# Attention: the products of probabilities and values of a batch, taken one step later

## The chip, the core and the metric

The kernel runs on one core of a Trainium2 chip. That core has TensorE (PE, the matrix engine, with its weight loads shown apart as PEld), VectorE (DVE), ScalarE (ACT), GpSimd (POOL) and SyncE (SP, which here only issues DMAs). Each engine takes its own instructions strictly in the order in which the program wrote them, and waits on semaphores that other engines raise. The metric is the device time in microseconds (us) of one execution; the time of a kernel is the median of several executions.

## The reference

Four parts run one after another on `x` of 16 batches x 512 rows x 256 columns: attention with a layer norm and a residual, a mixture-of-experts feed-forward, a Mamba mixer, and the feed-forward again. Only the attention is touched:

```python
Q = x @ Wq.T + bq;  K = x @ Wk.T + bk;  V = x @ Wv.T + bv        # x is the normed input
theta_q = Q * inv_wl + phase_bias;  theta_k = K * inv_wl + phase_bias
sim = cos(theta_q) @ cos(theta_k).T + sin(theta_q) @ sin(theta_k).T
weights = softmax(sim / sqrt(256), axis=-1)
out = weights @ V                                                # x + out goes on
```

## The kernel before

The function `attention` handles the 16 batches one after another. There is no planner: for each engine a function `emit(st)` writes the instructions of one step, and `run_steps` calls it for steps -3, -2, ... and then in a loop. In the step of batch b, `st.has(1)` guards work for batch b+1, `st.has(2)` for b+2 and so on; `st.has(0)` is the batch itself. So the order of the sections inside `emit` is the order of the queue of that engine. The stages of a batch are:

- **Load and norm.** SP loads `xin` (L163). DVE takes the statistics (L270 to L277), POOL the power -0.5 (L188), DVE writes the normed `xn` (L301). These are done three steps ahead.
- **Transposes.** PE transposes `xn` into the banks `ps_t` (L412), DVE splits them into a high and a low part `xT_hi`, `xT_lo` (L261, L264). Two steps ahead, at the end of the step on PE.
- **Projections.** PE makes four blocks of queries and keys (L376) and two blocks of values (L384), one after another in two PSUM banks that take turns, `ring[0]` and `ring[1]`. ACT empties the first four into `theta` (L319), DVE the last two into `vals` (L229). Block three needs the bank that ACT has emptied of block one. One step ahead, at the start of the step on PE.
- **Angles.** DVE reduces `theta` into one turn with five passes (L236 to L251). ACT then makes sine, absolute value and cosine (L341, L342, L345) and two rounded copies `trig_hi` (L347, L350), and POOL and DVE the two remainders `trig_lo` (L194, L219). One step ahead up to the copies.
- **Similarities.** PE makes four blocks of `ps_s` with 48 matmuls (L401). ACT takes the exponential of each into `probs` (L329), in the order: the four `theta` of batch b+1, the four exponentials of batch b, the sines and copies of batch b+1.
- **Probabilities times values.** PE makes four blocks `ps_o` (L424), each of 257 columns, in two banks that take turns; the last column is the sum of the probabilities. DVE divides and adds the residual (L288, L290), SP stores (L173).

On PE the step of batch b is: projections of b+1, similarities of b, transposes of b+2, products of b. In text below, "block three" is the third block of projections, and "the products" are always the matmuls of L424. `probs`, `vals`, `xres`, `xout`, `trig_hi` and `trig_lo` each have two buffers. The attention is followed by the first feed-forward, which starts when the last batch is stored.

Of the kernel before, what the change touches and what calls it, by code (L numbers as in the profile page):

```python
# [54 lines left out]
def attention(nc, x, wqkT, wvT, bqk, bv, phase, inv_wl, ident, x1):  # L55
# [8 lines left out]
    C1 = 6.28125  # L64
    C2 = 2.0 * math.pi - C1
    PI_IN = 3.1415925
    with ExitStack() as ctx:
        def sb(name, shape, dt=F32):
            return ctx.enter_context(nc.sbuf_tensor("a_" + name, shape, dt))
# [78 lines left out]
        def _(sp):  # L148
# [8 lines left out]
            def emit(st):  # L157
                if st.has(3):
                    h, n = st.half(3), st.turn(3)

                    if st.reuses(3):
                        sp.wait_ge(xn_ready, TT * (st.item(3) - 1))
                    sp.dma_start(xin[h][:, :, :], rows(x, st.item(3))).then_inc(xin_loaded[h], 16)  # L163
                if st.has(0):
                    h, n = st.half(0), st.turn(0)

                    if st.reuses(0):
                        sp.wait_ge(out_free[1], 2 * (st.item(0) - 1))
                    sp.dma_start(xres[h][:, :, :], rows(x, st.item(0))).then_inc(xres_loaded[h], 16)

                    for r in range(2):
                        sp.wait_ge(out_free[r], 2 * st.item(0) + 2)
                    sp.dma_start(rows(x1, st.item(0)), xout[h][:, :, :]).then_inc(stored[h], 16)  # L173

            run_steps(sp, emit, NB, 3)
            for h in range(2):
                sp.wait_ge(stored[h], 16 * (NB // 2))

# [21 lines left out]
        def _(dve):  # L200
# [13 lines left out]
            def emit(st):  # L214
                if st.has(0):

                    h, b = st.half(0), st.item(0)
                    dve.wait_ge(trig_high, 2 * b + 2)
                    nc.vector.tensor_tensor(trig_lo[h][:, NF:2 * NF, :], trig[:, NF:2 * NF, :],  # L219
                                            trig_hi[h][:, NF:2 * NF, :].bitcast(F32),  # L220
                                            ALU.subtract).then_inc(cos_low, 1)
                if st.has(1):
                    h, n, b = st.half(1), st.turn(1), st.item(1)

# [41 lines left out]
                if st.has(3):  # L266
# [6 lines left out]
                    for t in range(TT):  # L273
# [2 lines left out]
                    dve.wait_ge(mv_done, b + 1)  # L276
                    nc.vector.tensor_scalar(var_eps[h][:, :], mv[h][:, :, 1], EPS, None,  # L277
                                            ALU.add).then_inc(var_done, 1)
                if st.has(0):
                    h, n, b = st.half(0), st.turn(0), st.item(0)  # L280
                    dve.wait_ge(xres_loaded[h], 16 * (n + 1))

                    if st.reuses(0):
                        dve.wait_ge(stored[h], 16 * n)
                    for t in range(TT):
                        r = t % 2
                        dve.wait_ge(out_full[r], 2 * b + t // 2 + 1)
                        nc.vector.reciprocal(rden[:, t:t + 1], ps_o[r][:, D:D + 1]).then_inc(rden_done, 1)  # L288
                        dve.wait_ge(rden_done, TT * b + t + 1)
                        ins = nc.vector.scalar_tensor_tensor(out=xout[h][:, t, :], in0=ps_o[r][:, 0:D],  # L290
                                                             scalar=rden[:, t:t + 1], in1=xres[h][:, t, :],
                                                             op0=ALU.mult, op1=ALU.add)
                        ins.then_inc(out_free[r], 1)
                if st.has(3):
                    h, n, b = st.half(3), st.turn(3), st.item(3)
                    dve.wait_ge(rstd_done, b + 1)
# [5 lines left out]
                                                      rstd[h][:, t:t + 1], ALU.subtract, ALU.mult)  # L302
                        ins.then_inc(xn_ready, 1)

            run_steps(dve, emit, NB, 3)

        @block.scalar
        def _(act):
# [47 lines left out]
        def _(pe):  # L356
# [9 lines left out]
            def emit(st):  # L366
                if st.has(1):
# [11 lines left out]
                    for v in range(2):  # L379
                        r = take(st, NF + v)  # L380
                        for u in range(2):
                            t = 2 * v + u
                            for i, (wp, xp, k) in enumerate(parts):
                                ins = nc.tensor.matmul(ring[r][:, u * D:(u + 1) * D],  # L384
                                                       xp[:, k, t * P:(t + 1) * P], wp[:, k, 2 * D:3 * D],
                                                       start=(i == 0), stop=(i == len(parts) - 1))
                        ins.then_inc(ring_full[r], 1)
                if st.has(0):
                    h, n, b = st.half(0), st.turn(0), st.item(0)

# [13 lines left out]
                if st.has(2):  # L404
                    h, b = st.half(2), st.item(2)
                    pe.wait_ge(xn_ready, TT * (b + 1))
                    for k in range(KT):
# [4 lines left out]
                            ins = nc.tensor.transpose(ps_t[k][:, t * P:(t + 1) * P],  # L412
                                                      xn[h][:, t, k * P:(k + 1) * P], id_sb[:, :])
                        ins.then_inc(xT_full, 1)
                if st.has(0):
                    h, b = st.half(0), st.item(0)
                    pe.wait_ge(probs_ready, TT * (b + 1))
                    for r in range(2):
                        pe.wait_ge(ring_free[r], 3 * b + 3)
                    for s in range(TT):  # L420
                        r = s % 2
                        pe.wait_ge(out_free[r], 2 * b + s // 2)
                        for t in range(TT):
                            ins = nc.tensor.matmul(ps_o[r][:, 0:D + 1], probs[h][:, t, s * P:(s + 1) * P],  # L424
                                                   vals[h][:, t, :], start=(t == 0), stop=(t == TT - 1))
                        ins.then_inc(out_full[r], 1)

            run_steps(pe, emit, NB, 3)

AXIS = mybir.AxisListType
# [1348 lines left out]
```

## Time and profile before

| | |
|---|---|
| median of 3 executions | 3050.72 us (3048.64 to 3051.18) |
| profiled execution, its own time | 3049.55 us |
| its span | 3047.7 us |
| mean granted clock of TensorE | 0.949 of full speed |
| attention | from the start to about 508 us |
| PE busy over the whole span | 2680.0 us (88%) |
| DVE, ACT, POOL busy over the whole span | 2345.8, 1847.0, 1824.2 us |

A row of the timeline gives start, duration, engine, line, operation, output<-input, shape and count; a bracket at its end is the idle time of the engine before it and what ended it. L401 is line 401 of the kernel before. A matmul of f32 operands counts as two in the records (an `x16` of L424 is eight matmuls of the program).

### The profile page before, as it was taken

What the parts mean: (1) busy time and instruction counts of PE and PEld (TensorE: products, weight loads), DVE (VectorE), ACT (ScalarE), POOL (GpSimd) and SP (SyncE); (2) the same over time, 40 slices, a digit from 0 to 9 for tenths busy, and PEclk for the clock granted to TensorE, in tenths of its full rate; (3) what the DMA queues carried; (4) which work ended last, traced back from release to release, by engine and by line L of the source; (5) the groups of instructions that cost most, each with busy time, mean ns of one, the idle gap of its engine ahead of it and who ended that gap; (6) DMA issues with size and microseconds to landing.
All of it is one profiled execution on the core that took longest, in us unless ns stands there. A gap on an engine that the chain in (4) does not pass through costs nothing. (4 is left out here: it accounts for less than half of the span.)

```text
span 3047.7 us, 48452 instructions
## 1 busy us (share of the span) xinstructions
PE 2680.0 (88%) x17374; PEld 2139.6 (70%) x17374; DVE 2345.8 (77%) x2432; ACT 1847.0 (61%) x2523; POOL 1824.2 (60%) x1211
## 2 busy tenths in 40 slices
PE   5999995795389999999999999999999999985793
PEld 4877874563158788788787787787887877874562
DVE  6888874463259898898988998988989989895563
ACT  3565562252178677776776776676777767761451
POOL 1221220454148778777777787787877877784454
PEclk8999998798599999999999999999999999997896
DMA  1121213323222021120220210202202202103423
GB/s 48 63 62 41 62 49 73 108 77 89 77 70 63 15 84 43 42 84 8 77 85 1 84 59 26 84 14 72 84 2 83 70 15 77 43 29 80 119 77 100
DMA packets 137178, 186.01 MB, mean 61 GB/s; under 512 B 27848, under 2 KB 112712, under 8 KB 136968
## 3 DMA queue, kind: packets, MB, share of 16 engines
q1 hardware_dynamic: 129480, 162.68, 17.3%
q0 software_dynamic: 7488, 20.46, 2.6%
q8 instruction: 141, 2.31, 0.3%
q14 instruction: 69, 0.57, 0.1%
HBM read 141.12 MB, written 41.98 MB: 60 GB/s over the span
## 5 line engine op out<-in xcount | busy, mean ns | idle before, releaser
L1287 POOL TENSOR_TENSOR m_state<-m_state,m_c_all 128x1024 f32<-128x1024 f32 x512 | 1204.5, 2366 | 358.8 <-DVE m_state L1379 357.7
L1379 DVE TENSOR_TENSOR_SCAN m_state<-m_decay,m_ps_d 128x1024 f32<-128x1024 f32 x512 | 1161.9, 2278 | 149.9 <-issue 88.8
L1447 ACT ACTIVATE m_decay<-m_dt,m_aneg 128x511 f32<-128x511 f32 x1024 | 657.6, 710 | 27.4 <-DVE m_state L1379 26.6
L1671 PEld LDWEIGHTS m_ps_d<-m_bdiag,m_duT 128*128 128x128 f32 x4096 | 491.8, 193 | 109.8 <-issue 77.3
L1671 PE MATMUL m_ps_d<-m_bdiag,m_duT 128*128 128x128 f32 x4096 | 508.1, 278 | 33.3 <-DVE m_state L1379 23.7
L1684 PE MATMUL m_ps_y<-m_ident,m_state 128*128 128x128 f32 x4096 | 534.2, 274 | 2.8 <-POOL m_state L1287 2.5
L1684 PEld LDWEIGHTS m_ps_y<-m_ident,m_state 128*128 128x128 f32 x4096 | 464.7, 142 | 8.4 <-POOL m_state L1287 7.3
L1356 DVE TENSOR_TENSOR m_duB<-m_duT,m_ps_i 128x1024 f32<-128x1024 f32 x256 | 306.0, 1195 | 7.7 <-ACT m_duT L1475 7.7
L1669 PEld LDWEIGHTS m_ps_d<-m_ident,m_duB 128*128 128x128 f32 x2048 | 235.6, 141 | 76.8 <-issue 70.8
L1669 PE MATMUL m_ps_d<-m_ident,m_duB 128*128 128x128 f32 x2048 | 265.8, 273 | 7.1 <-DVE m_state L1379 7.0
L1585 PE MATMUL m_ps_f<-m_hT,m_win 128*128 128x512 f32 x512 | 248.7, 610 | 18.9 <-DVE m_dt L1323 16.6
L1608 PE MATMUL m_ps_f<-m_up,m_tap 128*128 128x512 f32 x512 | 230.6, 593 | 0.0
L188 POOL TENSOR_TENSOR a_rstd<-a_var_eps,a_neg_half 128x4 f32<-128x4 f32 x16 | 16.2, 1010 | 297.4 <-DVE a_var_eps L277 297.4
L872 ACT ACTIVATE f_hid<-f_ps_up 128x1024 f32<-128x1024 f32 x92 | 94.3, 1025 | 124.5 <-PE f_ps_up L940 124.5
L1608 PEld LDWEIGHTS m_ps_f<-m_up,m_tap 128*128 128x128 f32 x512 | 92.6, 190 | 94.9 <-issue 94.9
L1488 ACT ACTIVATE m_u<-m_ps_f,m_cb 128x512 f32<-128x512 f32 x64 | 44.0, 687 | 184.4 <-PE m_ps_f L1608 184.1
L1585 PEld LDWEIGHTS m_ps_f<-m_hT,m_win 128*128 128x128 f32 x512 | 89.7, 195 | 92.7 <-issue 66.2
L1488 ACT ACT_TABLE_LOAD x64 | 82.1, 1283 | 89.6 <-PE m_ps_f L1608 72.0
L424 PE MATMUL a_ps_o<-a_vals,a_probs 128*128 128x257 f32 x512 | 118.9, 385 | 16.3 <-DVE a_xout L290 14.5
L194 POOL TENSOR_TENSOR a_trig_lo<-a_trig,a_trig_hi 128x2048 fp32r<-128x2048 f32 x16 | 73.7, 4606 | 96.5 <-ACT a_trig_hi L347 96.5
L1269 POOL TENSOR_TENSOR m_sp_l<-m_sp_l,m_sp_a 128x512 f32<-128x512 f32 x64 | 81.8, 1277 | 77.9 <-ACT m_sp_a L1467 77.9
L329 ACT ACTIVATE a_probs<-a_ps_s 128x512 f32<-128x512 f32 x64 | 38.3, 599 | 138.3 <-PE a_ps_s L401 138.3
(194 smaller groups left out, 4417.4 us busy)
## 6 DMA issues: line engine op xcount, KB each, us to landing
m_c_all<-m_c_rows SPq DMA_DIRECT2D x128, 512.0 KB, 5.3
out<-m_xw SPq DMA_DIRECT2D x32, 512.0 KB, 3.1
f_y_rows<-f_y_sb SPq DMA_DIRECT2D x46, 256.0 KB
a_xin<-x SPq DMA_DIRECT2D x16, 512.0 KB, 4.8
a_xres<-x SPq DMA_DIRECT2D x16, 512.0 KB, 5.7
x<-a_xout SPq DMA_DIRECT2D x16, 512.0 KB, 3.3
m_xin<-x SPq DMA_DIRECT2D x16, 512.0 KB, 5.3
m_xw<-out SPq DMA_DIRECT2D x16, 512.0 KB, 5.4
```

The source lines that it names most:

```text
L424: ins = nc.tensor.matmul(ps_o[r][:, 0:D + 1], probs[h][:, t, s * P:(s + 1) * P], vals[h][:, t, :], start=(t == 0), stop=(t == TT - 1))
L872: nc.scalar.activation(hid[q][:, :, :], ps_up[q][:, :, :], ACT.Gelu).then_inc(gelu_done, 1)
L1287: nc.gpsimd.tensor_tensor(s, s, c_all[:, n, :, :], ALU.mult).then_inc(weighed, 1)
L1356: nc.vector.tensor_tensor(duB[:, r, :, :, :], duT[:, c, :, :].unsqueeze(1).to_broadcast([P, 2, TT, P]), ps_bt[h][:, 2 * n:2 * n + 2, :].un ...
L1379: nc.vector.tensor_tensor_scan(state[:, r, :, :].rearrange("p n t -> p (n t)"), decay[:, r, :, :].rearrange("p n t -> p (n t)"), ps_d[i % ...
L1447: ins = nc.scalar.activation(decay[:, r, j, 1:S], dt_sb[:, c, 1:S], ACT.Exp, scale=aneg[:, c, n:n + 1])
L1488: nc.scalar.activation(dst[h][:, c, :], f_bank(kind, c)[:, :], ACT.Silu, bias=bias).then_inc(done, 1)
L1585: ins = nc.tensor.matmul(f[:, :], win[:, k, e * P:(e + 1) * P], hT[:, k, :], start=(k == 0), stop=(k == KT - 1))
L1608: ins = nc.tensor.matmul(f[:, :], tap[:, k, s, :], up[:, k % 2, s:s + S], start=(s == 0), stop=(s == K - 1))
L1669: ins = nc.tensor.transpose(drive_t, duB[:, i // 2 % SR, j, t, :], id_sb[:, :])
L1671: ins = nc.tensor.matmul(drive_t, duT[:, c, t, :], bdiag[:, n // 2, TT * j + t, :], start=True, stop=True)
L1684: ins = nc.tensor.matmul(ps_y[:, t, :], state[:, i % RING, j, t * P:(t + 1) * P], id_sb[:, :], start=(n == 0 and j == 0 and t == 0), stop= ...
```

## The change

On PE the products of batch b are no longer written at the end of the step of batch b, but in the next step, behind the projections and ahead of the similarities. Since each step makes the projections one batch ahead, those of batch b+2 now stand ahead of the products of b. DVE's division and residual of batch b move with them into the next step, behind the cosine remainder and ahead of `vals`; SP's store moves too. Because there is now work one batch behind, `run_late` takes the place of `run_steps`: it has one step more at the end (with nothing but the products of batch 15), and seven steps instead of five ahead of the loop. ACT and POOL keep their programs.

```diff
+    def run_late(eng, emit):
+
+        for n in range(-3, 4):
+            emit(Step(n // 2, n % 2, NB))
+        pairs = (NB - 3) // 2
+        with eng.Fori(2, pairs) as i:
+            emit(Step(i, 0, NB))
+            emit(Step(i, 1, NB))
+        for n in range(2 * pairs, NB + 1):
+            emit(Step(n // 2, n % 2, NB))
...
+                if st.has(-1):
+                    h = st.half(-1)
                     for r in range(2):
-                        sp.wait_ge(out_free[r], 2 * st.item(0) + 2)
-                    sp.dma_start(rows(x1, st.item(0)), xout[h][:, :, :]).then_inc(stored[h], 16)
+                        sp.wait_ge(out_free[r], 2 * st.item(-1) + 2)
+                    sp.dma_start(rows(x1, st.item(-1)), xout[h][:, :, :]).then_inc(stored[h], 16)
...
                                             ALU.subtract).then_inc(cos_low, 1)
+                if st.has(-1):
+                    h, n, b = st.half(-1), st.turn(-1), st.item(-1)
+                    dve.wait_ge(xres_loaded[h], 16 * (n + 1))
...
+                    for t in range(TT):
+                        r = t % 2
+                        dve.wait_ge(out_full[r], 2 * b + t // 2 + 1)
+                        nc.vector.reciprocal(rden[:, t:t + 1], ps_o[r][:, D:D + 1]).then_inc(rden_done, 1)
...
+                        ins.then_inc(out_free[r], 1)
                 if st.has(1):
...
-                if st.has(0):
-                    h, n, b = st.half(0), st.turn(0), st.item(0)
-                    dve.wait_ge(xres_loaded[h], 16 * (n + 1))
...
-                        ins.then_inc(out_free[r], 1)
                 if st.has(3):
...
                         ins.then_inc(ring_full[r], 1)
+                if st.has(-1):
+                    h, b = st.half(-1), st.item(-1)
+                    pe.wait_ge(probs_ready, TT * (b + 1))
+                    for r in range(2):
+                        pe.wait_ge(ring_free[r], 3 * b + 3)
+                    for s in range(TT):
+                        r = s % 2
+                        pe.wait_ge(out_free[r], 2 * b + s // 2)
+                        for t in range(TT):
+                            ins = nc.tensor.matmul(ps_o[r][:, 0:D + 1], probs[h][:, t, s * P:(s + 1) * P],
+                                                   vals[h][:, t, :], start=(t == 0), stop=(t == TT - 1))
+                        ins.then_inc(out_full[r], 1)
                 if st.has(0):
...
                         ins.then_inc(xT_full, 1)
-                if st.has(0):
-                    h, b = st.half(0), st.item(0)
-                    pe.wait_ge(probs_ready, TT * (b + 1))
...
-                        ins.then_inc(out_full[r], 1)
-
-            run_steps(pe, emit, NB, 3)
-
+
+            run_late(pe, emit)
```

What stands in the row on PE from the end of one step to the start of the next, before (`a_ps_s` are the similarities, `a_ps_t` the transposes, `a_ps_o` the products, `a_ring` the projections):

```order
L401 MATMUL a_ps_s<-a_trig_hi,a_trig_lo 128x512 x4
L412 MATMUL a_ps_t<-a_ident,a_xn 128x128 x8
L424 MATMUL a_ps_o<-a_vals,a_probs 128x257 x16
L376 MATMUL a_ring<-a_xT_hi,a_w_hi 128x512 x2
L376 MATMUL a_ring<-a_xT_hi,a_w_lo 128x512 x2
```

The same place of PE with the change:

```order
L427 MATMUL a_ps_s<-a_trig_hi,a_trig_lo 128x512 x4
L438 MATMUL a_ps_t<-a_ident,a_xn 128x128 x8
L390 MATMUL a_ring<-a_xT_hi,a_w_hi 128x512 x2
L390 MATMUL a_ring<-a_xT_hi,a_w_lo 128x512 x2
L390 MATMUL a_ring<-a_xT_lo,a_w_hi 128x512 x2
```

The sixteen products have gone from between the transposes and the projections. The other place on PE, from the value projections to the similarities, before:

```order
L384 MATMUL a_ring<-a_w_hi,a_xT_hi 128x256 x2
L384 MATMUL a_ring<-a_w_lo,a_xT_hi 128x256 x2
L384 MATMUL a_ring<-a_w_hi,a_xT_lo 128x256 x2
L401 MATMUL a_ps_s<-a_trig_hi 128x512 x4
L401 MATMUL a_ps_s<-a_trig_lo,a_trig_hi 128x512 x4
```

And with the change:

```order
L398 MATMUL a_ring<-a_w_hi,a_xT_hi 128x256 x2
L398 MATMUL a_ring<-a_w_lo,a_xT_hi 128x256 x2
L398 MATMUL a_ring<-a_w_hi,a_xT_lo 128x256 x2
L411 MATMUL a_ps_o<-a_vals,a_probs 128x257 x16
L427 MATMUL a_ps_s<-a_trig_hi 128x512 x4
L427 MATMUL a_ps_s<-a_trig_lo,a_trig_hi 128x512 x4
```

The products now stand between the value projections of the batch ahead and the similarities of the batch after theirs. On DVE, from the statistics to `vals`, before:

```order
L277 TENSOR_SCALAR a_var_eps<-a_mv 128x4
L288 RECIPROCAL a_rden<-a_ps_o 128x1
L290 SCALAR_TENSOR_TENSOR a_xout<-a_ps_o,a_rden,a_xres 128x256
L288 RECIPROCAL a_rden<-a_ps_o 128x1
L290 SCALAR_TENSOR_TENSOR a_xout<-a_ps_o,a_rden,a_xres 128x256
L288 RECIPROCAL a_rden<-a_ps_o 128x1
L290 SCALAR_TENSOR_TENSOR a_xout<-a_ps_o,a_rden,a_xres 128x256
L288 RECIPROCAL a_rden<-a_ps_o 128x1
L290 SCALAR_TENSOR_TENSOR a_xout<-a_ps_o,a_rden,a_xres 128x256
L301 TENSOR_SCALAR a_xn<-a_xin,a_mv,a_rstd 128x256 x4
L219 TENSOR_TENSOR a_trig_lo<-a_trig,a_trig_hi 128x2048
L229 TENSOR_TENSOR a_vals<-a_ring,a_b_v 128x2x256 x2
```

With the change:

```order
L306 TENSOR_SCALAR a_var_eps<-a_mv 128x4
L315 TENSOR_SCALAR a_xn<-a_xin,a_mv,a_rstd 128x256 x4
L233 TENSOR_TENSOR a_trig_lo<-a_trig,a_trig_hi 128x2048
L245 RECIPROCAL a_rden<-a_ps_o 128x1
L247 SCALAR_TENSOR_TENSOR a_xout<-a_ps_o,a_rden,a_xres 128x256
L245 RECIPROCAL a_rden<-a_ps_o 128x1
L247 SCALAR_TENSOR_TENSOR a_xout<-a_ps_o,a_rden,a_xres 128x256
L245 RECIPROCAL a_rden<-a_ps_o 128x1
L247 SCALAR_TENSOR_TENSOR a_xout<-a_ps_o,a_rden,a_xres 128x256
L245 RECIPROCAL a_rden<-a_ps_o 128x1
L247 SCALAR_TENSOR_TENSOR a_xout<-a_ps_o,a_rden,a_xres 128x256
L258 TENSOR_TENSOR a_vals<-a_ring,a_b_v 128x2x256 x2
```

The division and residual have gone from ahead of `xn` and the cosine remainder to behind both, and now stand ahead of `vals` and of the five passes that follow it.

## Rows read from the trace of the kernel before

**Rows 1.** Busy time of the engines, 75 to 475 us; then PE's waits there.
```profile
core 0: us, PE busy (x) PEld busy (x) DVE busy (x) ACT busy (x) POOL busy (x), PEclk, DMA share, GB/s
75.00:475.00 400.00, 384.30 (x1887) 321.01 (x1886) 320.28 (x434) 238.14 (x209) 76.74 (x26) 1.00 0.17 53
...
PE a_ps_o L424 <- DVE a_xout L290: 13.2, 12, 1.2
```

**Rows 2.** Timeline of PE, one step in the loop, similarities of batch 3 to 4.
```profile
142.24 1.09 PE L401 MATMUL a_ps_s<-a_trig_hi 128*128 128x512 f32 x4
...
153.15 1.03 PE L412 MATMUL a_ps_t<-a_ident,a_xn 128*128 128x128 f32 x8
...
158.98 3.75 PE L424 MATMUL a_ps_o<-a_vals,a_probs 128*128 128x257 f32 x16 [1.07 <-DVE a_xout L290]
...
162.37 0.82 PE L376 MATMUL a_ring<-a_xT_hi,a_w_hi 128*128 128x512 f32 x2
...
165.36 0.70 PE L376 MATMUL a_ring<-a_xT_hi,a_w_hi 128*128 128x512 f32 x2
...
171.06 1.08 PE L401 MATMUL a_ps_s<-a_trig_hi 128*128 128x512 f32 x4
```

**Rows 3.** Timeline of ACT in the same step.
```profile
153.35 0.60 ACT L329 ACTIVATE a_probs<-a_ps_s 128x512 f32<-128x512 f32 x1 [2.12 <-PE a_ps_s L401]
...
155.26 1.91 ACT L341 ACTIVATE a_trig<-a_sin_in 128x2048 f32<-128x2048 f32 x1
...
164.52 0.76 ACT L319 ACTIVATE a_theta<-a_ring,a_shift,a_wl_c 128x512 f32<-128x512 f32 x1
```

**Rows 4.** Timeline of PE, the step after the loop, similarities of batch 14 last.
```profile
441.54 1.03 PE L412 MATMUL a_ps_t<-a_ident,a_xn 128*128 128x128 f32 x8
...
442.41 7.21 PE L424 MATMUL a_ps_o<-a_vals,a_probs 128*128 128x257 f32 x32
...
449.27 0.82 PE L376 MATMUL a_ring<-a_xT_hi,a_w_hi 128*128 128x512 f32 x2
...
453.72 0.73 PE L376 MATMUL a_ring<-a_xT_hi,a_w_hi 128*128 128x512 f32 x2 [1.29 <-ACT a_theta L319]
...
459.44 1.09 PE L401 MATMUL a_ps_s<-a_trig_hi 128*128 128x512 f32 x4
```

**Rows 5.** Timeline of DVE in the step of rows 2.
```profile
141.87 1.28 DVE L229 TENSOR_TENSOR a_vals<-a_ring,a_b_v 128x512 f32<-128x512 f32 x2
...
143.07 1.21 DVE L236 TENSOR_SCALAR a_turns<-a_theta 128x2048 f32<-128x2048 f32 x1
...
150.24 1.23 DVE L251 TENSOR_SCALAR a_sin_in<-a_rest 128x2048 f32<-128x2048 f32 x1
...
154.99 1.28 DVE L264 TENSOR_TENSOR a_xT_lo<-a_ps_t,a_xT_hi 128x512 fp32r<-128x512 f32 x2
```

**Rows 6.** Timeline of all engines, the last two batches.
```profile
471.20 7.23 PE L424 MATMUL a_ps_o<-a_vals,a_probs 128*128 128x257 f32 x32 [0.69 <-ACT a_probs L329]
...
478.67 0.48 DVE L290 SCALAR_TENSOR_TENSOR a_xout<-a_ps_o,a_rden,a_xres 128x256 f32<-128x256 f32 x1
...
481.84 4.90 DVE L219 TENSOR_TENSOR a_trig_lo<-a_trig,a_trig_hi 128x2048 fp32r<-128x2048 f32 x1 [2.69 <-ACT a_trig_hi L350]
486.88 2.04 PE L401 MATMUL a_ps_s<-a_trig_hi 128*128 128x512 f32 x4 [8.46 <-DVE a_trig_lo L219]
...
490.11 1.07 PE L401 MATMUL a_ps_s<-a_trig_hi,a_trig_lo 128*128 128x512 f32 x4
```

**Rows 7.** PE at the start of the program, then one window.
```profile
40.81 1.22 PE L376 MATMUL a_ring<-a_xT_hi,a_w_hi 128*128 128x512 f32 x2 [10.61 <-DVE a_xT_lo L264]
...
45.25 0.95 PE L376 MATMUL a_ring<-a_xT_lo,a_w_hi 128*128 128x512 f32 x2
...
49.59 1.05 PE L376 MATMUL a_ring<-a_xT_lo,a_w_hi 128*128 128x512 f32 x2
...
52.91 0.39 PE L384 MATMUL a_ring<-a_w_hi,a_xT_hi 128*128 128x256 f32 x2
...
50.00:51.00 1.00, 1.00 (x4) 0.79 (x3) 1.00 (x1) 0.31 (x1) 0.56 (x1) 0.50 0.05 16
```

More of the change, by code:

```diff
@@ L169, in emit @@
                     sp.dma_start(xres[h][:, :, :], rows(x, st.item(0))).then_inc(xres_loaded[h], 16)
+                if st.has(-1):
+                    h = st.half(-1)
                     for r in range(2):
-                        sp.wait_ge(out_free[r], 2 * st.item(0) + 2)
-                    sp.dma_start(rows(x1, st.item(0)), xout[h][:, :, :]).then_inc(stored[h], 16)
-            run_steps(sp, emit, NB, 3)
+                        sp.wait_ge(out_free[r], 2 * st.item(-1) + 2)
+                    sp.dma_start(rows(x1, st.item(-1)), xout[h][:, :, :]).then_inc(stored[h], 16)
+            run_late(sp, emit)
             for h in range(2):
@@ L221, in emit @@
                                             ALU.subtract).then_inc(cos_low, 1)
+                if st.has(-1):
+                    h, n, b = st.half(-1), st.turn(-1), st.item(-1)
+                    dve.wait_ge(xres_loaded[h], 16 * (n + 1))
+                    if st.reuses(-1):
+                        dve.wait_ge(stored[h], 16 * n)
+                    for t in range(TT):
+                        r = t % 2
+                        dve.wait_ge(out_full[r], 2 * b + t // 2 + 1)
+                        nc.vector.reciprocal(rden[:, t:t + 1], ps_o[r][:, D:D + 1]).then_inc(rden_done, 1)
+                        dve.wait_ge(rden_done, TT * b + t + 1)
+                        ins = nc.vector.scalar_tensor_tensor(out=xout[h][:, t, :], in0=ps_o[r][:, 0:D],
+                                                             scalar=rden[:, t:t + 1], in1=xres[h][:, t, :],
+                                                             op0=ALU.mult, op1=ALU.add)
+                        ins.then_inc(out_free[r], 1)
                 if st.has(1):
@@ L278, in emit @@
                                             ALU.add).then_inc(var_done, 1)
-                if st.has(0):
-                    h, n, b = st.half(0), st.turn(0), st.item(0)
-                    dve.wait_ge(xres_loaded[h], 16 * (n + 1))
[L283 to L292, printed above, removed]
-                        ins.then_inc(out_free[r], 1)
                 if st.has(3):
@@ L303, in emit @@
                         ins.then_inc(xn_ready, 1)
-            run_steps(dve, emit, NB, 3)
+            run_late(dve, emit)
         @block.scalar
@@ L414, in emit @@
                         ins.then_inc(xT_full, 1)
-                if st.has(0):
-                    h, b = st.half(0), st.item(0)
-                    pe.wait_ge(probs_ready, TT * (b + 1))
[L418 to L425, printed above, removed]
-                        ins.then_inc(out_full[r], 1)
-            run_steps(pe, emit, NB, 3)
+            run_late(pe, emit)
 AXIS = mybir.AxisListType
```

## The prediction

> **What bounds the kernel now.** Only the attention is touched, so I left the whole-program page quickly and read the stretch from 75 to 475 us by itself. The view of busy time by window says that PE is busy 384.3 of 400 us there [rows 1], and the list of waits says that nearly all of what is left is one wait, the third block of the products waiting for DVE to empty the first: 12 records of about 1.1 us, 13.2 us together [rows 1]. From these two alone one would call the attention bound by PE, and a change that removes this wait a gain of some 13 us.
>
> The timeline of one step says something else [rows 2, 3]. Let 0 be the end of the similarities of batch 3 (153.15). ACT takes the last exponential at 153.35 to 153.95, changes its table, begins the sines of batch 4 at 155.26 and is done with the whole chain (sine, absolute value, cosine, two copies) at 164.52, where the first `theta` of batch 5 starts. It ends at 164.52 + 0.76 = 165.28, and PE starts block three at 165.36, which needs the bank that this `theta` emptied. So block three starts 165.36 - 153.15 = 12.21 us after the similarities end, and ACT has no gap in between: that is a chain. The proof that the 12.21 us are ACT's and not PE's is the step after the loop [rows 4]. There the products run without the wait in the middle (32 records without a break), so the projections begin early, at 449.27, and then PE stands 1.29 us, until `theta` releases it at 453.72. The similarities ended there at 441.54, and block three starts 453.72 - 441.54 = 12.18 us later: the same distance. PE saved its 1.1 us and handed them back.
>
> The period of a step is thus three pieces: 10.91 us of similarities (142.24 to 153.15), 12.21 us from their end to block three, and 5.70 us from block three to the next similarities (165.36 to 171.06), together 28.82 [rows 2]. The step after the loop has 5.72 for the last piece [rows 4]. PE's products, transposes and first two blocks lie beside ACT's chain and cost nothing.
>
> **What the change moves.** The products leave the 12.21 us in which they were free and go into the piece between block three and the similarities, which was on the chain. PE does them in 449.27 - 442.41 = 6.86 us [rows 4]. The switch from them to the next kind of matmul may cost a little: the first pair behind products lasts 0.82 us (162.37), the first pair behind a wait 0.73 (453.72) [rows 2, 4]. I allow 0.2, so 7.05 us for a step (bounds 6.86 and 7.25). It happens in the steps of batches 1 to 14, since those have both projections ahead and products behind: 14 x 7.05 = 98.7 us.
>
> What do we get back? The chain on ACT has no program change, and it starts at the same event (the last exponential), so 12.21 stays. The wait in the middle of the products, 1.07 us [rows 2], was off the path, and its removal is worth nothing. With the products gone, PE has only the transposes (1 us) in that time, then waits for DVE's split, which ended at 154.99 + 1.28 = 156.27, that is 3.1 us after 0 [rows 5], does blocks one and two by 6.1, and stands until 12.2: about 8.2 us idle in a step, in two parts of 2.1 and 6.1 us.
>
> DVE's moved work: the four divisions and residuals are now ahead of `vals` and the five passes. In the tail the products end at 471.20 + 6.86 = 478.06 and DVE's last residual at 478.67 + 0.48 = 479.15, 1.1 us after them [rows 6]. Then `vals` takes 143.07 - 141.87 = 1.20 and the five passes 150.24 + 1.23 - 143.07 = 8.40 [rows 5]: `sin_in` is ready 10.7 us after the similarities begin. ACT wants it at 155.26 - 142.24 = 13.02 [rows 2, 3]. A slack of 2.3 us, so cost nothing; without that slack each us would cost 14. The cosine remainder (L219) now runs beside POOL's and may take 4.9 us [rows 6] instead of 2.28: from 11.4 to 16.3 us after 0, while the products begin only at 12.2 + 5.7 = 17.9. Nothing there. `xn` goes earlier, away from POOL; nobody waits for it. SP's loads of `xin` and `xres` now stand behind a store that waits 7 us longer or so, but they feed work a whole step away; cost nothing.
>
> **The clock.** PE's idle stretch costs twice. The granted clock was 1.00 throughout 75 to 475 us [rows 1], with idle of about 1.1 us a step. At the start of the program, after 10.61 us idle, PE ran at the lower level, 1.2 of 2.4 GHz: ten matmuls from 40.81 to 45.25 take 4.44 us, where 12 take 2.99 at the higher [rows 2, 7], so 4.44 - 10 x 0.249 = 1.95 lost. After a further idle stretch of 2.3 us, with six matmuls' time behind it, it was low again (0.50 in the window [rows 7]): eight in 3.32 us (49.59 to 52.91), 1.33 lost. After 8.46 us idle in the tail, eight took 490.11 - 486.88 = 3.23 where they take 8 x 10.91 / 48 = 1.82 [rows 2, 6], 1.41 lost. In the new step PE is busy for only 2.9 of the 11.1 us ahead of block three, so I expect the low level at block three in nearly every step, all of it on the chain. The three losses are between 1.3 and 2.4 (the first with its two remaining matmuls); I take 1.8, so 14 x 1.8 = 25 us, with bounds 0 and 34.
>
> The Trainium skill says under "HAM oscillation — how this bites in real kernels" (TensorE: Matmul & The Clock Gate) that a kernel with such a gap in every tile pays the transition in every tile, and in the section on the gate that the loss is about half of the throttled time. The trace agrees with the second: 3.32 us low cost 1.33. By the page an estimate would be 14 x 1.6 = 23 us instead of 25.
>
> **The end.** In the step of batch 15 there are no projections: PE has the products of 14, then the similarities of 15. But DVE now takes the cosine remainder of 15 first, which ends at 481.84 + 4.90 = 486.74, and only then empties the first block of the products. So blocks three and four, which ran long before, now start at about 486.74 + 0.75 = 487.5 and take 3.4 us, and the similarities follow at about 491 instead of 486.88: +4.1 us. The bounds are 3 and 6 (at the lower clock). The last batch's products keep their cost.
>
> **The sum.** 98.7 + 25 + 4 = 128 us, on the profiled execution's own 3049.55: 3177.6; the median lies 1.2 higher: 3178.7, say 3178. Own range: 3152 (no loss of clock) to 3190.
>
> **The rivals.**
> 1. *The products go on the path, the clock stays high.* For it: two blocks are done in the middle of the gap. Against: all three comparable gaps fell. 98.7 + 4 = 103: 3153.
> 2. *PE is the bound after all, and the kernel is faster.* For it: 96% busy [rows 1]. If PE's queue were the limit, taking out the wait in the middle of the products would give 14 x 1.1 = 15 us: 3035. It decides if block three need not wait for the sines, that is, if `theta` of a batch could come out of `ring` ahead of the sines of the last. ACT's order forbids that. The Trainium skill says under "Identifying the Most-Contended Engine" (Perfetto Trace Analysis) that matmul busy time is no good measure for TensorE and the weight loads' is better. The row for those, 321 of 400, is 80%, and speaks against PE as the bound.
> 3. *DVE's reduction becomes late.* If the residual, `vals` and the five passes take more than 13.02 us after the similarities begin, ACT waits for `sin_in`. The slack is 2.3 us; passes slowed by POOL would eat it, but POOL's long one is over by then. With 1.5 us in each step: 3178 + 21 = 3199.
> 4. *The change does nothing to the time.* It would have to hide the 6.86 us in a gap of PE between block three and the similarities, and there is none in rows 2. 3050.
>
> **How the numbers follow.** Forecast 0.75, rival 1 0.12, rival 2 0.03, rival 3 0.08, rival 4 0.02. The range takes in rival 1 and part of rival 3: 3150 to 3193. A measurement can tell about 0.2% (6 us) from no change. Faster 0.03, same 0.02, slower 0.95.
>
> **What would show it.** The sines of two successive batches start 28.8 us apart now; they should be 35.9 apart, plus the clock's 1 to 2.4. PE should stand some 6 us ahead of block three in each step, waiting for ACT's `theta` (about 85 us in 14 waits), and 2 us ahead of block one, waiting for DVE's split. The wait of the products for DVE should be gone but for one long one at the end, about 12 us. The granted clock over the steps should be below 1.00, with block three's six matmuls at 0.43 us apiece. The attention should end at about 508 + 128 = 636 us, and all behind it take the same time. The prediction is wrong if the period is near 28.8 (ACT's chain was no chain), or if ACT waits for `sin_in`.

## The result and the profile after

| | before | after |
|---|---|---|
| median | 3049.68 us (3045.63 to 3051.18, 4 executions) | 3167.43 us (3166.07 to 3169.91, 4 executions) |
| ratio, 95% interval | | 1.0389 (1.0371 to 1.0407) |
| profiled execution, its span | 3049.55, 3047.7 | 3166.07, 3164.3 |
| mean granted clock | 0.949 | 0.938 |

The forecast was 3178 with a range of 3150 to 3193; the time is 10.6 us below it. (Of the experiments below, one execution of new_half took 4285.76 us at a mean granted clock of 0.621; its ratio leaves that one out, its median does not.) The busy time by window, 75 to 475 us, in the columns of [rows 1]:

```profile
75.00:475.00 400.00, 316.82 (x1464) 264.21 (x1465) 240.94 (x345) 178.78 (x158) 59.85 (x21) 0.91 0.14 44
```

PE was busy 384.3 of 400 us before [rows 1] and is busy 316.8 now, at a granted clock of 0.91 where it was 1.00. So PE, which looked like the bound, now stands idle for 83 of 400 us. The list of waits says for whom (75 to 600 us; total us, times, longest):

```profile
PE a_ring L390 <- ACT a_theta L333: 82.1, 14, 5.9
PE a_ring L390 <- DVE a_xT_lo L293: 28.8, 13, 2.3
PE a_ps_o L411 <- ACT a_probs L343: 0.7, 1, 0.7
```

The wait of the products for DVE, 13.2 us in 12 records before [rows 1], is gone here (one long one comes at the end, below). In its place block three waits 14 times for `theta`, 5.9 us each, and block one 13 times for the split. The timeline of PE over one step (from the end of one batch's similarities to the end of the next), which answers [rows 2]:

```profile
180.79 0.73 PE L390 MATMUL a_ring<-a_xT_hi,a_w_hi 128*128 128x512 f32 x2 [2.29 <-DVE a_xT_lo L293]
...
189.64 1.22 PE L390 MATMUL a_ring<-a_xT_hi,a_w_hi 128*128 128x512 f32 x2 [5.78 <-ACT a_theta L333]
190.66 1.05 PE L390 MATMUL a_ring<-a_xT_hi,a_w_lo 128*128 128x512 f32 x2
...
197.11 7.12 PE L411 MATMUL a_ps_o<-a_vals,a_probs 128*128 128x257 f32 x32
...
203.88 1.28 PE L427 MATMUL a_ps_s<-a_trig_hi 128*128 128x512 f32 x4
...
214.98 1.03 PE L438 MATMUL a_ps_t<-a_ident,a_xn 128*128 128x128 f32 x8
...
227.16 1.22 PE L390 MATMUL a_ring<-a_xT_hi,a_w_hi 128*128 128x512 f32 x2 [5.88 <-ACT a_theta L333]
```

Read it as four pieces: 214.98 to 227.16 is the 12.18 us from the end of the similarities to block three; 189.64 to 197.11 is 7.47 for the rest of the projections, where it was 5.70 [rows 2]; 197.11 to 203.88 is 6.77 for the products; 203.88 to 214.98 is 11.10 for the similarities, where it was 10.91. Together 37.52. The granted clock in three windows of the same step says why the second piece is longer:

```profile
184.00:185.00 1.00, 0.00 (x0) 0.00 (x0) 1.00 (x4) 1.00 (x1) 0.00 (x0) 1.00 0.00 0
...
188.00:189.00 1.00, 0.00 (x0) 0.00 (x0) 0.04 (x1) 1.00 (x2) 1.00 (x1) 0.50 0.00 0
...
192.00:193.00 1.00, 1.00 (x4) 0.81 (x3) 1.00 (x1) 0.39 (x1) 0.00 (x0) 0.50 0.00 0
```

It is still 1.00 just after PE begins to stand, is 0.50 at the end of the gap, and still 0.50 3 us after block three has started (full speed is 2.4 GHz, 0.50 is 1.2). The timeline of ACT in the same step, which answers [rows 3]:

```profile
215.18 0.60 ACT L343 ACTIVATE a_probs<-a_ps_s 128x512 f32<-128x512 f32 x1 [2.12 <-PE a_ps_s L427]
215.79 1.28 ACT L355 ACT_TABLE_LOAD   x1
217.09 1.91 ACT L355 ACTIVATE a_trig<-a_sin_in 128x2048 f32<-128x2048 f32 x1
...
226.35 1.43 ACT L333 ACTIVATE a_theta<-a_ring,a_shift,a_wl_c 128x512 f32<-128x512 f32 x2
```

From the last exponential to the first `theta` it has no gap, as before: 226.35 - 214.98 = 11.37, to the hundredth what it was (164.52 - 153.15, [rows 2, 3]). The sines start 37.36 to 37.57 us apart from the second on (28.80 to 28.89 before).

The end of the attention, which answers [rows 6]:

```profile
601.91 4.89 DVE L233 TENSOR_TENSOR a_trig_lo<-a_trig,a_trig_hi 128x2048 fp32r<-128x2048 f32 x1 [12.00 <-ACT a_trig_hi L364]
...
606.92 0.48 DVE L247 SCALAR_TENSOR_TENSOR a_xout<-a_ps_o,a_rden,a_xres 128x256 f32<-128x256 f32 x1
...
607.46 6.63 PE L411 MATMUL a_ps_o<-a_vals,a_probs 128*128 128x257 f32 x16 [12.44 <-DVE a_xout L247]
...
613.74 1.27 PE L427 MATMUL a_ps_s<-a_trig_hi 128*128 128x512 f32 x4
```

Here the products stand 12.44 us in their middle, for a division that DVE makes only after the cosine remainder.

The two spans differ by 116.6 us. The load of the feed-forward's identity matrix marks the end of the attention; it starts at 513.75 us before and at 638.91 after, so the attention has 125.2 more; the rest of the program takes 2534.0 before and 2525.4 after, 8.6 less, though none of its code was changed. The forecast put the attention at 128 more and the rest at 0.

### The profile page after: what moved, and what is told of

Read it like the earlier page. It is cut to its first block and busy times, and to the rows that moved or that the text cites. A ratio compares the mean times of both kernels' runs of the same rounds, so it can differ in the third digit from the quotient of the medians.

```text
span 3164.3 us, 48408 instructions
## 1 busy us (share of the span) xinstructions
PE 2696.5 (85%) x17374; PEld 2153.3 (68%) x17374; DVE 2333.6 (74%) x2432; ACT 1845.9 (58%) x2523; POOL 1823.9 (58%) x1211
## 5 line engine op out<-in xcount | busy, mean ns | idle before, releaser
L1684 PE MATMUL m_ps_d<-m_bdiag,m_duT 128*128 128x128 f32 x4096 | 504.5, 276 | 30.9 <-DVE m_state L1392 23.6
L390 PE MATMUL a_ring<-a_xT_hi,a_w_hi 128*128 128x512 f32 x128 | 58.1, 545 | 128.0 <-ACT a_theta L333 84.3
L1501 ACT ACT_TABLE_LOAD x64 | 82.1, 1283 | 89.6 <-PE m_ps_f L1621 72.0
L233 DVE TENSOR_TENSOR a_trig_lo<-a_trig,a_trig_hi 128x2048 fp32r<-128x2048 f32 x16 | 78.8, 4924 | 73.0 <-ACT a_trig_hi L364 73.0
```

What stands on the lines that cost most here:

```text
L1501: nc.scalar.activation(dst[h][:, c, :], f_bank(kind, c)[:, :], ACT.Silu, bias=bias).then_inc(done, 1)
L1684: ins = nc.tensor.matmul(drive_t, duT[:, c, t, :], bdiag[:, n // 2, TT * j + t, :], start=True, stop=True)
```

## The experiments

There are twelve more kernels. Times are medians, beside executions of the kernel before on the same chip. Since "the rest" moves with every kernel (see pad16), the column "attention" is the start of that load of the identity matrix, less the 513.75 us of the kernel before. Both columns come from one trace of each kernel.

| kernel | time, that of before | ratio (95%) | attention | rest |
|---|---|---|---|---|
| the change | 3167.43, 3049.68 | 1.0389 (1.0371 to 1.0407) | +125.2 | 2525.4 |
| old_half | 3045.01, 3044.15 | 1.0002 (0.9989 to 1.0014) | +2.0 | 2530.5 |
| new_half | 3146.02, 3044.15 | 1.0333 (1.0312 to 1.0353) | +74.8 | 2555.1 |
| copy_on_dve | 3142.5, 3044.15 | 1.0321 (1.0304 to 1.0339) | +103.1 | 2526.8 |
| filler | 3148.29, 3044.15 | 1.0349 (1.0332 to 1.0367) | +112.7 | 2518.3 |
| out_first | 3084.67, 3048.19 | 1.0119 (1.0100 to 1.0138) | +33.2 | 2535.5 |
| values_first | 3058.18, 3048.19 | 1.0032 (1.0020 to 1.0044) | +11.5 | 2530.9 |
| mid_gap | 3063.24, 3048.19 | 1.0048 (1.0030 to 1.0067) | +26.8 | 2521.3 |
| tail_fix | 3162.07, 3048.19 | 1.0372 (1.0355 to 1.0389) | +123.9 | 2520.7 |
| pad16 | 3039.6, 3047.27 | 0.9975 (0.9965 to 0.9985) | +0.8 | 2526.3 |
| pad44 | 3038.7, 3047.27 | 0.9971 (0.9960 to 0.9982) | +0.6 | 2522.5 |
| dve_both | 3024.18, 3047.27 | 0.9923 (0.9909 to 0.9936) | -22.8 | 2533.1 |
| old_sin_on_dve | 3045.25, 3047.27 | 0.9996 (0.9987 to 1.0006) | -2.3 | 2530.9 |

### Were the products free before, and are they on the chain now?

**old_half** and **new_half** have one edit, which leaves out two of the four blocks of keys of the products, each on its own kernel:

```diff
-                        for t in range(TT):
+                        for t in range(TT // 2):
                             ins = nc.tensor.matmul(ps_o[r][:, 0:D + 1], probs[h][:, t, s * P:(s + 1) * P],
-                                                   vals[h][:, t, :], start=(t == 0), stop=(t == TT - 1))
+                                                   vals[h][:, t, :], start=(t == 0), stop=(t == TT // 2 - 1))
```

> The kernel before, with half of the products left out (two of the four blocks of keys in L424; the output is not the reference's): 3.4 us less of TensorE in each of 16 steps. Theory (ScalarE's chain of 12.2 us from the end of the similarities to block three sets the step, the products lie beside it): the sines stay 28.8 us apart, 3050 us, unless the longer idle of TensorE (two parts of 3.0 and 1.6 us a step) lets its clock fall, which would add up to 1.7 us a step, 3074 at most. Rival (TensorE, 96% busy, is the bound): 15 x 3.4 = 51 us less, 2999.

> The changed kernel with the same half of the products left out. Theory (the products now stand on the chain): 14 x 3.43 = 48 us less than 3167, so 3119, and the sines 34.1 apart instead of 37.5. Rival (the loss comes from DVE's or ScalarE's new place, or from the clock alone, not from the products' length): within 6 us of 3167.

In the kernel before, 3.4 us less work of PE in each step did not make it faster: ratio 1.0002, sines 28.8 apart in twelve of the 15 periods. PE gave the time back: its wait for DVE in the middle of the products grew from 1.1 to 2.8 us, and in five steps it then stood 1.4 to 1.5 us ahead of block three, waiting for `theta`. The other three periods were 1.2 to 1.5 us longer than before (31.57, 30.07 and 30.34); in the second of them the products behind the 2.8 us took 3.80 us instead of 2.00, with the granted clock at 0.50 up to block one's end. In the changed kernel the same cut takes 50.4 us from the attention (588.5 against 638.9), where 48 were forecast, and the sines are 34.1 to 34.2 apart instead of 37.5. That settles the main point: the same products cost nothing where they stood and their full length where they stand now. The ratio of the whole went only from 1.0389 to 1.0333, since the rest of new_half took 29.7 us more than that of the changed kernel; this is taken up under pad16.

**copy_on_dve** shortens ScalarE's chain:

```diff
-                    act.wait_ge(trig_in_used, 3 * b + 3)
-                    nc.scalar.activation(trig_hi[h][:, NF:2 * NF, :], trig[:, NF:2 * NF, :], ACT.Copy)\
-                        .then_inc(trig_high, 1)
...
+                    dve.wait_ge(trig_in_used, 3 * b + 3)
+                    dve.wait_ge(trig_high, 2 * b + 1)
+                    if st.reuses(0):
+                        dve.wait_ge(sim_full, TT * (b - 1))
+                    nc.vector.tensor_copy(trig_hi[h][:, NF:2 * NF, :], trig[:, NF:2 * NF, :]).then_inc(trig_high, 1)
                     dve.wait_ge(trig_high, 2 * b + 2)
```

> The changed kernel with the second rounded copy (1.9 us, L364) taken from ScalarE and given to VectorE, which is idle there. Theory (ScalarE's chain bounds the step): 1.9 us less in 14 steps and at both ends, about 27 to 30 less: 3138. Rival (TensorE or VectorE is the bound): no change, 3167, or slower by VectorE's added pass of 1.2 to 3 us.

The attention lost 22.1 us, where 27 to 30 were forecast, and the sines are 35.35 and 36.33 apart in turn (37.5 less 1.9 is 35.6). So ScalarE's chain is what the step waits for. The wait for `theta` fell from 82.1 to 46.5 us in 14 times, more than 1.9 a step, since every second step blocks one and two now ran at the lower clock too.

### What the clock costs

**filler** keeps PE at work in the gap:

```diff
                     for f in range(NF):
+                        if f == 2 and st.has(-1):
+                            pe.wait_ge(out_free[0], 2 * st.item(-1))
+                            for q in range(24):
+                                nc.tensor.matmul(ps_o[0][:, :], w_hi[:, q % 2, 0:P], xT_hi[h][:, q % 2, :],
+                                                 start=True, stop=True)
                         r = take(st, f)
```

> The changed kernel with 24 matmuls more in each step between block two and block three (into a bank of the products that is free then; nothing reads them), about 5.6 us of the 5.9 us in which TensorE stands. It takes nothing off the path. Theory (1.7 us a step are lost since the granted clock is 0.50 at block three): the clock stays at 1.00, 14 x 1.67 = 23 us less: 3144, and the sines 35.9 apart. Rival (the clock is not what costs, the 1.7 us are a longer wait or a switch between kinds of matmul): 3167 or above.

The attention lost 12.5 us, about half of the 23 forecast. The timeline of PE shows both halves:

```profile
180.31 1.11 PE L395 MATMUL a_ring<-a_xT_hi,a_w_hi 128*128 128x512 f32 x2 [2.29 <-DVE a_xT_lo L293]
...
184.74 5.76 PE L391 MATMUL a_ps_o<-a_xT_hi,a_w_hi 128*128 128x512 f32 x24
190.34 0.63 PE L395 MATMUL a_ring<-a_xT_hi,a_w_hi 128*128 128x512 f32 x2
...
195.97 7.12 PE L416 MATMUL a_ps_o<-a_vals,a_probs 128*128 128x257 f32 x32
```

From block three to the products it is 195.97 - 190.34 = 5.63 us, against 7.47 without the filler: the 1.8 us were the clock's, and matmuls that nobody reads buy them back. But behind the idle 2.29 us ahead of block one the clock was now low (pairs of 0.85 us, 181.22 to 182.07), so blocks one and two took 4.43 us (180.31 to 184.74) instead of 2.9, and with the filler behind them block three started 13.36 us after the similarities instead of 12.2. The sines are 35.8 apart in four of 14 periods and 36.7 to 36.9 in the others, where 35.9 was forecast.

### Is it the place on PE or the step late?

**mid_gap** keeps the products a step late and puts them between blocks two and three. With DVE's residual moved ahead of the cosine remainder its core is

```diff
                     for f in range(NF):
+                        if f == 2:
+                            products(st)
                         r = take(st, f)
```

> The changed kernel, with the products of the batch before put between block two and block three of the projections, that is into the gap where TensorE waits for ScalarE, and DVE's residual ahead of the cosine remainder. Theory (the place on TensorE decides, not the step in which the products are made): they take 6.9 of the 5.9 us gap, so block three starts 13 us after the similarities instead of 12.2 and the clock stays high; sines 29.8 apart, about 108 us less than the changed kernel, 14 us above the kernel before. Rival (making them a step late costs by itself, by DVE's or SP's order): still 50 us or more above the kernel before.

Of the 125.2 us in the attention, 98.4 are gone (5 of them at the end, where DVE's residual now stands ahead of the cosine remainder); 26.8 stay, where 14 were forecast, and the ratio to the kernel before is 1.0048. So making the products a step late is nearly harmless; their place on PE was the loss. The part that was not forecast is the clock again. Two windows of 3 us, blocks one and two and then the products:

```profile
163.00:166.00 3.00, 3.00 (x8) 2.32 (x7) 1.77 (x10) 2.97 (x2) 1.01 (x1) 0.50 0.02 5
166.00:169.00 3.00, 3.00 (x15) 2.60 (x14) 0.92 (x4) 3.00 (x3) 0.57 (x1) 1.00 0.00 0
```

PE's 2.3 us for the split are now the only gap of a step, and still the clock is 0.50 behind it in most steps: ten of the last 14 periods are 31.1 to 31.3 long, the other four 29.6, as forecast (29.8). 10 x 1.55 for the clock and 14 x 0.8 for products that are longer than the gap come to 26.7.

**tail_fix** gives the residual precedence on DVE in the steps without projections:

```diff
+                for part in ((cosine_low, residual) if st.has(1) else (residual, cosine_low)):
+                    part()
```

> The changed kernel, with DVE's residual ahead of the cosine remainder only in the steps without projections (the last two). Theory: the wait of 12.4 us in the middle of the products of batch 14 goes, the similarities of batch 15 start as soon as the cosine remainder is there; 6.8 us less in the attention at the lower clock (613.7 to 606.9), the rest equal. Rival: nothing, as the remainder is later by the same time.

From the last sine to the load of the identity matrix it is 40.9 us, where the changed kernel has 46.4 and the kernel before 41.3. So 5.5 us come from the order at the end alone (6.8 were forecast). The attention as a whole is only 1.2 shorter, since its second sine came 2.7 us later and the three periods after it were 0.2 to 0.7 longer; why was not followed up.

### Was there anything to gain from the removed wait?

**out_first** takes away the wait in the middle of the products, in the kernel before: on DVE the section with `bn_stats` moves behind the one with `reciprocal`.

```diff
-                if st.has(3):
...
-                    for t in range(TT):
-                        nc.vector.bn_stats(stats[:, t, :], xin[h][:, t, :])
...
                 if st.has(0):
...
                         ins.then_inc(out_free[r], 1)
+                if st.has(3):
...
+                    for t in range(TT):
+                        nc.vector.bn_stats(stats[:, t, :], xin[h][:, t, :])
```

> The kernel before, with DVE's division and residual put ahead of the statistics of the batch three on. It takes away the 1.1 us for which the products waited in their middle, and nothing else. Theory (ScalarE's chain sets the step): TensorE gives the 1.1 us back at block three, the sines stay 28.8 apart, the time within 6 us of the kernel before. Rival (TensorE is the bound): 14 x 1.1 = 15 us less in the attention.

Neither time came: it is 1.2% slower. The timeline of one step:

```profile
161.17 1.03 PE L412 MATMUL a_ps_t<-a_ident,a_xn 128*128 128x128 f32 x8
...
173.16 4.61 POOL L194 TENSOR_TENSOR a_trig_lo<-a_trig,a_trig_hi 128x2048 fp32r<-128x2048 f32 x1
173.23 5.66 DVE L301 TENSOR_SCALAR a_xn<-a_xin,a_mv,a_rstd 128x256 f32<-128x256 f32 x4 [1.12 <-POOL a_rstd L188]
173.34 0.73 PE L376 MATMUL a_ring<-a_xT_hi,a_w_hi 128*128 128x512 f32 x2 [1.13 <-ACT a_theta L319]
...
178.81 2.28 DVE L219 TENSOR_TENSOR a_trig_lo<-a_trig,a_trig_hi 128x2048 fp32r<-128x2048 f32 x1
181.24 1.17 PE L401 MATMUL a_ps_s<-a_trig_hi 128*128 128x512 f32 x4 [2.01 <-DVE a_trig_lo L219]
```

The first half of the theory held: the products ran without a break, and PE gave their 1.1 us back ahead of block three, which starts 173.34 - 161.17 = 12.17 us after the similarities end and waits 1.13 us for `theta` (14.7 us in 13 times from 75 to 475 us). What was not seen is DVE. With the statistics behind the residual, `xn` waits 1.12 us for POOL's power and begins 12.06 us after the similarities (173.23 - 161.17). The cosine remainder comes behind it, and the similarities wait 2.01 us. The same two in the kernel before, in the step of [rows 2]:

```profile
163.37 5.25 DVE L301 TENSOR_SCALAR a_xn<-a_xin,a_mv,a_rstd 128x256 f32<-128x256 f32 x4
168.54 2.28 DVE L219 TENSOR_TENSOR a_trig_lo<-a_trig,a_trig_hi 128x2048 fp32r<-128x2048 f32 x1
```

There `xn` begins 163.37 - 153.15 = 10.22 us after the similarities, 1.8 earlier. It runs beside POOL's remainder in both kernels (5.25 and 5.66 us; it takes 1.4 where POOL has no remainder, in old_sin_on_dve), so that is no difference between them. The cosine remainder is done at 168.54 + 2.28 = 170.82, just ahead of the similarities at 171.06. So the kernel before had not one chain but three of nearly one length: ACT's, PE's and DVE's. In out_first the sines are 30.9 to 31.2 apart in ten periods; in three they are 32.5 to 32.7, and in the one shown the granted clock fell to 0.50 at 183 us, behind the 2.01 us.

**values_first** adds to out_first the value projections ahead of the others, so that less stands behind ACT's chain (on DVE `vals` goes ahead of the cosine remainder and `xn` behind it):

```diff
-                    for f in range(NF):
-                        r = take(st, f)
...
                     for v in range(2):
-                        r = take(st, NF + v)
+                        r = take(st, v)
...
+                    for f in range(NF):
+                        r = take(st, 2 + f)
```

> As out_first, and the two value projections are made ahead of the four of queries and keys (DVE's vals ahead of the cosine remainder, xn behind it). Behind the end of ScalarE's chain only blocks three and four are left (2.9 us) instead of 5.7, and the products stay where they were. Theory: ScalarE's chain stops being the bound, the step becomes TensorE's own work, 10.9 + 1.0 + 6.9 + 0.2 + 8.4 = 27.4, so the sines 27.4 to 27.8 apart and 15 x 1.2 = about 18 us less. Rival: the cosine remainder (ready 16.3 us after the similarities end) or the switch takes the gain, no change.

The rival held: 29.7 to 30.0 apart but for the first and the last period (27.6, as forecast), ratio 1.0032. The cosine remainder now ran beside POOL's from its start and took 6.1 to 6.7 us, and the similarities waited for it (16.0 us in 13 times from 75 to 450 us).

**dve_both** and **old_sin_on_dve** take the sine remainder from POOL, dve_both on top of values_first and with the statistics right behind `xn`, old_sin_on_dve alone in the kernel before:

```diff
-                    pool.wait_ge(trig_high, 2 * b + 1)
-                    nc.gpsimd.tensor_tensor(trig_lo[h][:, 0:NF, :], trig[:, 0:NF, :],
-                                            trig_hi[h][:, 0:NF, :].bitcast(F32), ALU.subtract).then_inc(sin_low, 1)
...
+                    dve.wait_ge(trig_high, 2 * b + 1)
+                    nc.vector.tensor_tensor(trig_lo[h][:, 0:NF, :], trig[:, 0:NF, :],
+                                            trig_hi[h][:, 0:NF, :].bitcast(F32), ALU.subtract).then_inc(sin_low, 1)
                     dve.wait_ge(trig_high, 2 * b + 2)
```

> As values_first, with the sine remainder on DVE too (GpSimd's pass of 4.6 us and with it the contention goes, DVE's two passes take 2.3 each), and the statistics behind xn. Theory (in values_first the similarities waited 0.9 us for a cosine remainder of 6.1 to 6.7 us beside GpSimd's, and the projections for vals): the remainder is ready 16 us after the similarities end, TensorE becomes the bound, the sines 27.4 to 27.8 apart, about 18 us less than the kernel before. Rival (the order on DVE, not GpSimd, made the remainder late): still 29 or more.

> The kernel before, with only the sine remainder moved from GpSimd to DVE. Theory: xn falls from 5.2 to 1.4 us and the remainders take 2.3 each, so DVE is no later than before, but ScalarE's chain and TensorE set the step: sines 28.8 apart, within 6 us of the kernel before. Rival (contention with GpSimd costs time on the path): 1 us or more less a step.

dve_both beats both kernels: ratio 0.9923 (0.9909 to 0.9936), the attention 22.8 us shorter, the sines 27.2 to 27.6 apart from the second on. Its window from 75 to 450 us:

```profile
75.00:450.00 375.00, 373.77 (x1853) 317.37 (x1852) 300.63 (x442) 235.75 (x207) 29.20 (x12) 1.00 0.18 56
```

PE is busy 373.8 of 375 us. This is what "PE is the bound" looks like; the 96% of [rows 1] was not it. The pass taken from POOL does not do it alone: old_sin_on_dve is at 0.9996, as forecast. Which of dve_both's other two edits are needed beside it was not tried one by one.

### The 8.6 us in code that was not changed

In the kernel before, PE stands for 1 us or more without waiting for another engine at five places in the Mamba part, one loop turn (some 241 us) apart; here three of them:

```profile
1347.49 2.05 PE L1671 MATMUL m_ps_d<-m_bdiag,m_duT 128*128 128x128 f32 x16 [1.32 <-issue]
...
1588.39 3.45 PE L1671 MATMUL m_ps_d<-m_bdiag,m_duT 128*128 128x128 f32 x16 [2.24 <-issue]
...
1831.09 3.68 PE L1671 MATMUL m_ps_d<-m_bdiag,m_duT 128*128 128x128 f32 x16 [2.43 <-issue]
```

The 16 matmuls behind the first stall take 2.05 us, those behind the two longer ones 3.45 and 3.68; the granted clock there is 1.00 from 1348 us and 0.50 from 1589. So a long stall costs twice, like the gap in the attention. In the changed kernel the stalls are shorter, and the turns 240.1 to 240.2 us apart instead of 240.9 to 242.7:

```profile
1470.98 2.05 PE L1684 MATMUL m_ps_d<-m_bdiag,m_duT 128*128 128x128 f32 x16 [1.03 <-issue]
...
1711.14 2.05 PE L1684 MATMUL m_ps_d<-m_bdiag,m_duT 128*128 128x128 f32 x16 [1.49 <-issue]
```

In new_half there are two in each turn, and the turns are some 246 apart:

```profile
1423.18 1.04 PE L1684 MATMUL m_ps_d<-m_bdiag,m_duT 128*128 128x128 f32 x7 [2.64 <-issue]
1427.06 2.08 PE L1684 MATMUL m_ps_d<-m_bdiag,m_duT 128*128 128x128 f32 x9 [2.84 <-issue]
```

**pad16** and **pad44** put matmuls that nobody reads into the kernel before, once, in the 10.6 us in which PE stands at the start:

```diff
+                if isinstance(st.base, int) and st.base == -1 and st.j == 1:
+                    for q in range(16):      # 44 in pad44
+                        nc.tensor.matmul(ps_o[0][:, :], w_hi[:, q % 2, 0:P], xT_hi[0][:, q % 2, :],
+                                         start=True, stop=True)
```

> The kernel before, with 16 matmuls more on TensorE, once, in the 10.6 us in which it stands at the start of the attention (nothing reads them, 3.7 us). They cost no time there. Theory on the 9 us that the rest of the program gained with the change (TensorE stands 1.0 to 2.8 us at each turn of the Mamba loop without waiting for an engine, by where its instructions happen to lie): the turn of the Mamba loop, 241.3 to 242.7 us apart before, changes by 1 us or more, and the stretch from the attention's end to the end of the program with it, by 5 us or more in either direction. Rival (the rest differs from run to run, or depends on when it starts): 2534 us as before, within 3.

> The same with 44 matmuls (10 us). Theory: again another time for a turn of the Mamba loop, not in proportion to the number. Rival: 2534 us within 3.

The attention is within 0.8 us of the kernel before, and yet both kernels are faster (0.9975 and 0.9971): the rest takes 2526.3 and 2522.5 instead of 2534.0, with stalls of 1.0 to 1.6 us in turns 239.6 to 240.0 apart. So the number of instructions far ahead, on the same engine, changes how long PE stands at the turn of a later loop. Why it does is open: no run separates the fetching of instructions from other causes. And the rest of a single execution says little to some us: the 24 executions of the kernel before beside pad16 lie between 3039.76 and 3054.88, so that the pads are faster rests on the ratios, and of the 8.6 us between the first two kernels, which have four executions each (7.4 by the medians: 117.75 less 125.16), a part may be such scatter.

## Why the prediction was right

- **The bound** (ACT's chain of 12.2 us, not PE). Right: 12.18 us after the change too, old_half shows that the work beside it was free, and copy_on_dve that a shorter chain on ACT shortens the step.
- **The products on the chain**, 7.05 us a step with 0.2 for the switch. Right: 6.77 us and 0.19 more in the similarities behind them, 6.96.
- **The wait in the middle is worth nothing.** Right, and for the stated reason: in out_first PE hands 1.13 us back at block three. What the prediction had not seen is that DVE's remainder was 0.24 us from the path, so that taking the wait away by DVE's order makes the kernel slower.
- **The clock**, 1.8 us a step. Right: 7.47 - 5.70 = 1.77, and filler takes it off in that place. That 2.3 us of idle can bring the clock down too, which filler and mid_gap then showed, was not in the forecasts of those two.
- **PE idle in two parts, 2.1 and 6.1.** 2.3 and 5.8.
- **DVE's moved work costs nothing** (slack 2.3 us). Right: `sin_in` is ready 10.6 us after the similarities begin (10.7 forecast) and the sines start at 13.2, with no wait of ACT for `sin_in` in these steps.
- **The end**, 4.1 us, bounds 3 and 6. From the last sine to the start of the last products it is 625.67 - 592.53 = 33.14 us, 27.56 before: +5.6. The size was low: blocks three and four of the products ran at the lower clock (607.46 to 613.74, 6.3 us instead of 3.4), of which 1.2 us came back, since the similarities behind them no longer began at the lower clock as before [rows 6]. The place was right, and tail_fix takes 5.5 off.
- **The sum.** 14 steps gave 121.5 us (123.7 forecast) and the end 5.6 (4.1). The first step gave -1.4 (no term; its blocks three and four lost time to the lower clock before, and not after the change), and from the last products to the load -0.5: together 125.2, forecast 128. The other 8.6 us are the rest of the program, where the prediction had "all behind it take the same time". That was wrong by 0.3%.
- **The rivals.** High clock: refuted by the windows. PE the bound: refuted by old_half. The weight loads' 80%, which the prediction held against PE, says little by itself: it is 85% (317.37 of 375 us) in dve_both, where PE never stands. DVE's reduction late: did not come. No change: refuted by the time.

## What to carry to other kernels

Split a period at the event that nobody can pass (here the end of the similarities) and ask of each piece which engine ended it; work in a piece that another engine ends is free, and moving it into the next piece costs its full length, and the clock with it if a gap opens. A busy share of 96% did not mean the bound: half of the products could go without any gain. Before removing a wait, look for other chains of nearly the same length: here out_first, values_first and old_sin_on_dve gained nothing, and dve_both, which changes DVE's order, PE's order and the contention together, gained 0.8%.

## What the runs showed of the hardware

- 2.2 to 2.3 us idle on TensorE brought its clock to 1.2 GHz in ten of 14 steps of mid_gap, where PE had worked without a break for 27 to 29 us; 1.8 to 2.1 us did so in three of 13 steps of out_first; idle of 1.1 us a step never did (1.00 over 400 us in the kernel before).
- `xn` (four passes of 128x256) takes 1.38 us on DVE alone and 5.1 to 5.8 beside GpSimd's subtraction; DVE's own subtraction of 128x2048 takes 2.28 alone and 4.9 to 6.7 when it begins beside it, while GpSimd's stays at 4.5 to 4.8. The sum of both remainders on DVE alone is 4.6 us, no more than GpSimd's one.
- The stall of PE at the turn of the Mamba loop was between 1.0 and 5.5 us a turn in 14 kernels with the same loop; 16 matmuls far ahead moved the whole program by 0.25%.
